# A slab's squares ahead of the unit's exponentials on ScalarE, in the first and third cross-attention of a four-layer decoder stack

## The reference, cut to what matters

```python
# layer 0: 32 query heads of 128, 8 key/value heads, RMS norm on q and k
q = rmsnorm(x_n @ Wq.T);  k = rmsnorm(ctx @ Wk.T);  v = ctx @ Wv.T
out = softmax(q k^T / sqrt(128)) v @ Wo.T
# layer 3: 32 query heads, 4 key/value heads, keys and values over [ctx, x_n]
out = softmax((x_n Wq)(h Wk)^T / sqrt(128)) (h Wv) @ Wo
```

## Time and profile before

| | us |
|---|---|
| median of three runs | 2218.27 |
| lowest, highest | 2217.47, 2220.11 |
| the profiled execution, its own time | 2218.68 |
| its span in the profile | 2216.9 |
| layer 0's periods 1 to 8 in the profile | about 90 to 605 |
| layer 3's periods 0 to 8 | about 1717 to 2168 |

### The profile page before, as it was taken

One profiled execution on the slowest core, in us unless ns is written; L12 is line 12 of the kernel. 1 busy time (PEld: TensorE's weight loads), 2 busy tenths in 40 slices (PEclk: granted clock), 3 DMA queues, 4 the chain that ended last, 5 costly groups with the idle time before them and its releaser, 6 DMA issues.

```text
span 2216.9 us, 39604 instructions
## 1 busy us (share of the span) xinstructions
PE 2058.8 (93%) x13732; PEld 1127.8 (51%) x13732; DVE 1346.0 (61%) x2722; ACT 1177.1 (53%) x3031; POOL 555.4 (25%) x958
## 2 busy tenths in 40 slices
PE   6799999999888899999999999998879899999998
PEld 3556565565544445555555555555334455555564
DVE  7577676676664846666666656656442466666664
ACT  6666667666532345555555555533222566666651
POOL 4233232332341412222222222113200222222221
PEclk9899999999999999999999999999989999999999
DMA  3222221221103113222232232211200233333311
GB/s 129 60 66 48 55 65 40 65 59 56 29 1 127 60 50 94 74 76 86 74 91 75 70 93 75 51 35 65 91 20 1 62 77 77 81 77 77 63 49 38
DMA packets 181336, 142.92 MB, mean 64 GB/s; under 512 B 158139, under 2 KB 166587, under 8 KB 171283
## 3 DMA queue, kind: packets, MB, share of 16 engines
q1 hardware_dynamic: 180690, 140.37, 22.9%
q10 hardware_dynamic: 448, 0.03, 0.0%
HBM read 100.26 MB, written 2.10 MB: 46 GB/s over the span
## 4 chain that ended last, share of the span: by engine, by line
PE 62%; DVE 15%; ACT 12%; issue 7%; POOL 2%; DMA 1%; DVEq 0%; ACTq 0%; POOLq 0%; SPq 0%
PE bank L85 19%; PE bank L86 18%; PE bank L87 18%; ACT m_E L563 3%; PE bank L2122 3%; DVE m_Sm L998 2%; ACT m_arena L431 2%; DVE m_x L1049 2%; ACT m_arena L542 2%; DVE m_A L1043 1%; DVE m_nmax L1015 1%; ACT m_arena L533 1%; ACT m_arena L534 1%; DVE m_arena L944 1%; DVE m_arena L949 1%
## 5 line engine op out<-in xcount | busy, mean ns | idle before, releaser
L944 DVE TENSOR_TENSOR m_arena<-bank,m_arena 128x512 f16<-128x512 f32 x320 | 221.4, 692 | 472.1 <-ACT m_arena L542 471.9
L85 PE MATMUL bank<-m_input_parts,m_arena 128*128 128x512 f16 x1120 | 429.7, 384 | 17.2 <-ACT m_input_parts L1683 5.4
L86 PE MATMUL bank<-m_input_parts,m_arena 128*128 128x512 f16 x1120 | 428.8, 383 | 0.0
L87 PE MATMUL bank<-m_input_parts,m_arena 128*128 128x512 f16 x1120 | 428.2, 382 | 0.0
L1061 POOL TENSOR_TENSOR m_E<-m_E,m_rinv 128x512 f32<-128x512 f32 (+1 forms) x192 | 172.2, 897 | 803.6 <-DVE m_rinv L1029 803.6
L563 ACT ACTIVATE m_E<-m_Sm,m_nmax 128x64 f32<-128x64 f32 (+1 forms) x512 | 185.4, 363 | 285.1 <-DVE m_nmax L1019 149.1
L542 ACT ACTIVATE m_arena<-bank 128x512 f16<-128x512 f32 x320 | 189.4, 592 | 234.4 <-PE bank L87 234.1
L86 PE MATMUL bank<-m_wo_t,m_A 128*128 128x512 f16 x768 | 292.3, 381 | 0.0
L85 PE MATMUL bank<-m_wo_t,m_A 128*128 128x512 f16 x768 | 292.2, 380 | 0.0
L87 PE MATMUL bank<-m_wo_t,m_A 128*128 128x512 f16 x768 | 292.0, 380 | 0.0
L85 PE MATMUL bank<-m_arena,m_input_parts 128*128 128x128 f16 (+1 forms) x768 | 187.5, 275 | 8.1 <-DVE m_arena L949 7.3
(11 more groups left out here) (308 smaller groups left out, 4155.1 us busy)
## 6 DMA issues: line engine op xcount, KB each, us to landing
m_raw<-a_q SPq DMA_DIRECT2D x24, 1024.0 KB, 5.0
m_raw<-a_o SPq DMA_DIRECT2D x24, 1024.0 KB, 5.0
m_raw<-a_k SPq DMA_DIRECT2D x9, 1024.0 KB, 4.9
m_raw<-a_v SPq DMA_DIRECT2D x9, 1024.0 KB, 5.0
m_bias_in<-bias SPq DMA_DIRECT2D x64, 128.0 KB, 2.1
m_arena<-f_w SPq DMA_DIRECT2D x3, 1024.0 KB, 7.7
m_PT<-m_split SPq DMA_TRANSPOSE x174, 3.0
m_x<-x SPq DMA_DIRECT2D x2, 1024.0 KB, 7.0
```

The costliest lines, as they stand in the source:

```text
L85: pe.matmul(out, lhs[0], rhs[0], start=first, stop=False)
L86: pe.matmul(out, lhs[0], rhs[1], start=False, stop=False)
L87: return pe.matmul(out, lhs[1], rhs[0], start=False, stop=last)
L944: ins = dve.tensor_tensor(self.dest(name, part, 1), self.shaped(name, bank[m % 2][:, :]), self.dest(name, part, 0), ALU.subtract)
```

## The change

In layer 0, in slots 0 and 4 of every period but the opening one, and in every slot of layer 3 that has squares (0 and 2), `w_squares` moves in the list from behind the first tile and the reciprocals to a place ahead of `scores`. Only ScalarE's emitter does anything with `w_squares`, so no other engine's order changes, and no wait, buffer or instruction is added or removed. On ScalarE the order in such a slot becomes: `split_hi` of the unit before, the squares, the four exponentials, the first tile's eviction, the second tile's, `mix`. Slots 1 and 5 of layer 0 and all of layer 2 stay as they were. What is moved: in layer 0 one slab in slot 0 of periods 1 to 7, one in slot 4 of periods 1 to 6, the y slab in period 8, 14 in all; in layer 3 two in each of periods 0 to 6 and one in period 7, 15 in all.

```diff
--- before.py
+++ after.py
@@ -193,6 +193,9 @@
                 out.append(("s_conv", 1))
             if normed == 3 and not first and made is None:
                 out.append(("k_read_hi", misc, slot // 4))
+            sooner = squared is not None and ((self.layer == 0 and slot in (0, 4) and not opening) or self.layer == 3)
+            if sooner:
+                out.append(("w_squares", squared))
             if ok(b) and normed != 2:
                 out.append(("scores", b))
             if fifth:
@@ -235,7 +238,7 @@
                 out.append(("rinv", b))
             if fifth:
                 out.append(("w_convert", 0))
-            if squared is not None:
+            if squared is not None and not sooner:
                 out.append(("w_squares", squared))
             keys = t == 8 and self.layer == 0
             if keys and slot < 2:
```

## The result

The changed kernel takes **2187.63 us** (median of three runs: 2179.80, 2187.63, 2188.33) against 2218.27 before: ratio 0.985, 95% interval 0.983 to 0.987. The forecast was 2183, with a range of 2176 to 2200. The profiled execution of after took 2187.63 us, with a span of 2185.8, at a mean granted clock of 0.977; that of before had 0.981.

A forecast was written before the change was run, and what follows sets the result against it. It took layer 0 as bound by a closed round of ScalarE and VectorE, layer 3 by TensorE. 20.6 + 1.9 + 7.8 + 0 + 5.4 = 35.7 us off 2218.7 gave 2183 us, range 2176 to 2200.

The forecast's parts named there:

- A: Layer 0's round of ScalarE and VectorE is shortened as forecast: 2183 us, from 2177 to 2190; chance 0.70.
- B: Rival: only the place of TensorE's wait moves, layer 0's round being held elsewhere: 2199 us; chance 0.16.
- C: Rival: more gain, layer 0's loop settles on TensorE's own supply: 2178 us, 2174 with a better clock; chance 0.06.
- D: Rival: slower, the later exponentials delay the path to `mix` and TensorE waits for `m_PT`: 2225 us; chance 0.05.
- E: Rival: the squares' own waits hold them in the new place until the old time: 2216 to 2219 us; chance 0.03.
- Step 1: Layer 0, slots 0 and 4 of periods 1 to 7: thirteen moved squares shorten the round, 20.6 us in all.
- The first square: Layer 0, period 1: the first moved square, where TensorE has no slack, worth 0.8 us, between 0 and 1.89.
- Step 2: Layer 0, period 8: moving the y slab's squares takes 1.9 us off TensorE's wait of 3.00 us in slot 1.
- Step 3: Layer 3, slot 2, periods 1 to 6: TensorE's six stalls at the sum go whole, 7.8 us.
- Step 4: Layer 3, slot 0, periods 1 to 7: no stall to remove, taken as 0, at most 3.5 us of loss.
- Step 5: Layer 3, period 0: with both slots' squares moved, the scores of slot 4 come 5.4 us earlier.
- The clock: Low granted clock behind stalls: neither gain nor loss counted, as layer 0's round hides it; 3 us of range.

The follow-up runs named there:

- experiment 5: Changed kernel with the 13 squares of layer 0's kinds o and q in periods 1 to 7 done twice in the new place: 2206.52 us.
- experiment 6: Kernel before, with the same 13 layer 0 squares in their old place but over a quarter of the slab: 2203.65 us.
- experiment 7: Changed kernel, but in layer 0's slots 0 and 4 the squares stand ahead of `split_hi`: 2182.65 us.
- experiment 1: The changed kernel measured once more, nothing altered: 2189.98 us.
- experiment 9: Changed kernel, but layer 3's slot 0 squares of periods 1 to 7 back in their old place: 2187.35 us.

## Why the prediction was right, and where it was off

**The mechanism, A, was right.** B's 2199 needed a round that did not shorten; half-periods went from 33.7 and 34.3 us to 32.1 and 32.7, and experiments 5 and 6 show that the round follows ScalarE's length from both sides. C's and D's conditions did not occur: stalls of 0.25 to 2.1 us are left behind L952, and no `mix` of layer 0 waits for `m_PT` in the trace. E's idle time ahead of the squares is not there.

**Step 1, 20.6 us.** Twelve of the thirteen squares lie between the sum in slot 2 of period 1 and that in slot 2 of period 7: 411.86 to 391.41 us, 20.5, where the forecast had 19.8 (10 x 1.60 + 2 x 1.89). From the o slab's sum of period 6 to that of period 7, with neither a turn nor a low clock in either trace, it is 68.03 to 64.78, 1.6 for each place as forecast. The first square, taken as 0.8 between bounds of 0 and 1.89, brought nothing: from the sum at 75.45 us to the k slab's, past its place, TensorE takes 32.50 us before and 32.54 in experiment 1. (The 1.5 us of the table stand in the opening; in the trace of experiment 1, of the same kernel, they are absent.) The remaining stall was put at 0.3 to 0.5 us and is 0.55 or 0.97 in most half-periods, with up to 2.1 where the loop turns. The delay of 0.29 us is there to the hundredth and in the round (experiment 7). K0's stalls are gone.

**Step 2, 1.9 us.** From slot 2 of period 1 TensorE has gained 20.5 us by 524.37 us, and 22.4 by 561.22, where a wait of 3.00 is now 2.58: the 1.9 came. Then it runs at the low clock (0.55 from 561 to 564), and 20.7 are left at 581.54. The step held, as experiment 9 confirms with 1.9 where the clock stays up; what the forecast lacked was a price for the clock behind it.

**Step 3, 7.8 us.** Six steady periods of layer 3 take 52.09 us in place of 53.42: 6 x 1.33 = 8.0.

**Step 4, 0.** Shown by experiment 9.

**Step 5, 5.4 us: the term that was too large.** The order gives 3.6: the first stall with its 0.15 (2.88), and 0.70 of the second (2.73 to 2.03). The 1.8 above that was the low clock inside Q1, which I took as gone with its stall though I wrote beside it that without it the sum would be about 4. It moved to the next stall. Where it stayed away (experiment 7), the second half took 4.34 us as forecast, and the whole came to 5.3.

**The clock, a term left at zero with 3 us of range.** With the middle counted to it, it made most of the difference of 4.6 us: 1.7 lost in period 8 of layer 0, 1.8 in period 0 of layer 3, 2.8 in the middle that the change doesn't touch (put down to the clock, not shown in full), and 1.5 gained in the opening, where before is at the low clock for about 17 us and after for about 14. How near 2187.6 comes to 2183 is in part luck: by the middle alone the traces differ by up to 6.7 us. The first square took 0.8 more; the other squares of layer 0 gave 0.7 more than forecast and layer 3's steady periods 0.2. The 1.8 could have been foreseen, the middle not. And one sentence of the forecast holds for before only: that in layer 0 the round hides the low clock. It does there (experiment 6). In the changed kernel TensorE's slack is used up, and period 5 with its piece at the low clock takes 1.5 us more than period 3; 0.8 of that is a longer stall ahead of the piece (2.12 us for 1.30), the rest may be the clock.

The rule of the Trainium skill that the forecast cited ("TensorE: Matmul & The Clock Gate", Part 1), that the gate's observation runs free of the kernel, agrees with the middle, where the same instructions get the low clock at other places in one trace than in another. No run here shows it, and the places aren't all different: in the five traces that have the changed order of layer 0 and nothing more there, the clock falls in period 5 each time.

## What to carry to other kernels

Look for the round before for the engine: ScalarE is busy 54% of the time, yet in layer 0 each microsecond that it works between the exponentials and the evictions is nearly one of the kernel's. The Trainium skill ("Perfetto Trace Analysis", Identifying the Most-Contended Engine) sends one to the engine with the highest occupancy first, and does not take the matmuls' busy share for a measure of how near TensorE is to its limit. That share is the highest here (94%), and it doesn't name the cause: the gaps of TensorE, followed to what ended them, led to the order on ScalarE. Put work that nobody waits for soon in the idle time ahead of the round's instruction that waits, and compare lengths: 1.9 us into 1.5 cost 0.3, and a second 1.9 us cost 1.8. A stall's price at TensorE is more than its length if the low clock follows it, but that part is not gained with the stall: it tends to come behind the next.

## What the runs showed of the hardware

- The same program spreads by its mean granted clock: before from 2215.6 us at 0.983 to 2224.9 at 0.976, the changed kernel from 2179.8 at 0.984 to 2190.2 at 0.977. The spread is wider than most of the differences between the experiments; the starts of equal instructions in the traces resolve tenths of a microsecond.
- In period 0 and the start of period 1 of layer 3 the clock fell behind a stall of 2.0 to 3.1 us in each profile, once or twice, but which of the stalls it chose went by no order that I can show. In layer 0 it stayed up behind a stall of 2.95 us in before and behind several of 2.8 us in experiment 5, and fell in the changed kernel behind one of 2.1: the length of the stall alone doesn't decide. What would keep it from falling was not tried.
- A square with accumulator over 128x2048 takes 1.90 us (1.89 to 1.93 in before and after), over 128x512 0.62, and each reads its accumulator for another 0.18 to 0.22 us.
- A piece at the low clock costs nothing that can be seen where TensorE has slack (before, layer 0, period 3) and 1.7 us where it has none (layer 3, period 0; layer 0, period 8).
